# A conv and expert-layer kernel: one image pair's x is added to the experts' sum on PE and copied out by ACT

## What is computed

```python
x = x + conv_ref(_ln_c(x), conv_w, conv_b)      # _ln_c: norm over the channels of a pixel
t = _to_tokens(x)                               # a token is a pixel's 64 channels
t = t + ffn_ref(_ln_t(t), router_w, router_b, expert_w, expert_b)
# conv_ref: x * sigmoid(conv3x3([max over channels, mean over channels]))
# ffn_ref:  softmax router, best 2 of 8 experts, their two outputs mixed by the two probabilities
```

## Time and profile before

| | us |
|---|---|
| median of 3 runs | 1394.77 (1394.36 to 1395.02) |
| the profiled execution | 1395.69 |
| its span, first to last instruction | 1393.8 |

### The profile page before, as it was taken

The page is one execution under the profiler, slowest core; times in us unless marked ns, Lnnn a source line. Parts: engine busy times, 40 slices in busy tenths (PEclk is TensorE's granted clock), DMA queues, the critical chain, the costliest instruction groups (busy, mean ns, idle before and its releaser), DMA issues.

```text
span 1393.8 us, 33104 instructions
## 1 busy us (share of the span) xinstructions
PE 1294.6 (93%) x11750; PEld 612.6 (44%) x11750; DVE 1240.0 (89%) x1527; ACT 1052.0 (75%) x3950; POOL 1066.0 (76%) x643
## 2 busy tenths in 40 slices
PE   8964999999999999999999999999999898889998
PEld 8853444444444444444444444444444332333332
DVE  6787799988999899998999799998999879998887
ACT  5677898888998889888898889888898533444442
POOL 5333787887888787877878878878878878789885
PEclk9955999999999999999999999999999999999999
DMA  6443466676666666576666666676666555657774
GB/s 224 120 123 89 132 207 206 174 224 199 198 187 213 194 204 199 173 226 199 199 200 199 199 200 200 187 217 192 207 203 175 163 166 162 175 167 205 205 204 144
DMA packets 85845, 259.97 MB, mean 187 GB/s; under 512 B 13744, under 2 KB 13744, under 8 KB 85680
## 3 DMA queue, kind: packets, MB, share of 16 engines
q1 hardware_dynamic: 85680, 257.85, 62.0%
HBM read 206.42 MB, written 51.38 MB: 185 GB/s over the span
## 4 chain that ended last, share of the span: by engine, by line
PE 56%; DVE 23%; issue 9%; POOL 2%; ACT 2%; DVEq 0%; POOLq 0%; ACTq 0%
PE moe L568 34%; DVE gx L714 13%; PE tm L493 8%; PE gb L514 8%; PE tm L507 2%; DVE ge L736 2%; DVE stats L691 2%; PE moe L562 2%; PE tm L553 2%; DVE ot L727 1%; DVE oh L749 1%; PE tm L592 1%; DVE u L799 1%; POOL dl L1265 1%; ACT sq L965 1%
## 5 line engine op out<-in xcount | busy, mean ns | idle before, releaser
L568 PE MATMUL moe<-gx,wc 128*64 128x448 f32 x3584 | 803.5, 551 | 0.0
L714 DVE TENSOR_TENSOR gx<-gb,xd 128x896 f32<-128x896 f32 x672 | 710.7, 1086 | 77.3 <-PE gb L514 72.9
L1205 POOL TENSOR_TENSOR gx<-gs,xd 128x896 f32<-128x896 f32 x224 | 492.8, 2200 | 228.0 <-ACT gs L1003 158.7
L965 ACT ACTIVATE sq<-xct 112x64 f32<-112x64 f32 x1400 | 338.4, 246 | 7.5 <-DVE early_s L701 2.1
L1003 ACT ACTIVATE gs<-gb 128x896 f32<-128x896 f32 x224 | 205.3, 916 | 176.4 <-PE gb L514 170.9
L568 PEld LDWEIGHTS moe<-gx,wc 128*64 128x64 f32 x3584 | 219.9, 136 | 201.6 <-issue 159.2
L965 ACT ACTIVATION_READ_ACCUMULATOR sq<-xct 112x1 f32 x1400 | 265.5, 190 | 0.0
L1222 POOL TENSOR_TENSOR tt<-xc,a1s 128x896 f32<-128x896 f32 x112 | 235.1, 2099 | 11.3 <-issue 9.7
L514 PE MATMUL gb<-s,cg 32*128 32x448 f16 x1792 | 175.6, 358 | 53.2 <-DVE gx L714 51.8
L514 PEld LDWEIGHTS gb<-s,cg 32*128 32x128 f16 x1792 | 48.0, 91 | 383.2 <-DVE gx L714 348.7
L493 PE MATMUL tm<-rhs,xa 64*112 64x74 f32 x2800 | 184.6, 272 | 10.6 <-ACT early_l L950 5.2
(11 more groups left out here) (94 smaller groups left out, 1090.0 us busy)
## 6 DMA issues: line engine op xcount, KB each, us to landing
xd<-in_x_dram SPq DMA_DIRECT2D x448, 224.0 KB, 4.0
xa<-in_x_dram SPq DMA_DIRECT2D x112, 448.0 KB, 4.5
xc<-in_x_dram SPq DMA_DIRECT2D x112, 448.0 KB, 4.8
out_dram<-ot SPq DMA_DIRECT2D x112, 448.0 KB, 3.6
gx<-in_const_g_dram SPq DMA_DIRECT2D x1, 384.0 KB, 5.5
cf<-in_const_f_dram SPq DMA_DIRECT2D x1, 333.5 KB, 3.1
cf<-in_L_ffn_expert_b_dram SPq DMA_DIRECT2D x12, 1.0 KB
gx<-in_L_ffn_expert_w_dram SPq DMA_DIRECT2D x1, 128.0 KB, 5.3
```

Source lines behind the costliest of these rows:

```text
L568: last = pe.matmul(moe[b * CH:(b + 1) * CH, c, 0:HALF], wc[:, k * CH:(k + 1) * CH], gx[:, u, b, :], start=False, stop=(k == KT - 1), skip_ ...
L714: dve.tensor_tensor(gx[:, i, :, :], gb[:, 2 * slot:2 * slot + 2, 0:HALF], xd[:, v % 2, :, c * HALF:(c + 1) * HALF], ALU.mult).then_inc(sca ...
L965: last = act.activation(sq[:, n, :], xct[:, step % 2, n, :], ACT.Square, accum_out=to[:, 1, lo + n:lo + n + 1])
L1205: pool.tensor_tensor(gx[:, ND + j, :, :], gs[:, j, :, :], xd[:, v % 2, :, j * HALF:(j + 1) * HALF], ALU.mult).then_inc(scaled_p, 1)
```

## The change

For the blocks of pair 6 alone (the 14 steps from `LONE` on), DVE's `finish` is left out, for both sums. PE gets one more step of accumulation into `moe` for each sum, right behind the last unit of the sum (unit 2, unit 5): a multiplication of `tt` with a unit matrix in f32, two matmuls of 128x64 by 448 columns, which wait for POOL's `tt`. ACT gets a copy of the finished sum from `moe` to `ot`, which waits for that addition: for the second sum of v-1 right behind the copy P1, for the first sum of v right behind the copy P0 of v+1, ahead of the sigmoid and of `a1s`. Those who waited for DVE's count (`store`, `biases`, `scale_x`) wait for ACT's in these blocks. The unit matrix is 128 more columns of f32 in the first constant load `cf`. All other pairs are as before.

```diff
+    f[:, o + P + 2:] = np.eye(P)
-        cf = sb("cf", [P, CC + 3 * W + E + P + 2])
+        cf = sb("cf", [P, CC + 3 * W + E + P + 2 + P])
+        unit = cf[:, bias_c + P + 2:bias_c + P + 2 + P]
...
+        LONE = (PAIRS - 2) * STEPS
+        def lone_step(r, v):
+            return (r - 2) * STEPS + v - LONE
+        def by_act(r, v):
+            return 0 <= lone_step(r, v) < STEPS
+        def finished(eng, r, v, n):
+            step = (r - 2) * STEPS + v
+            if by_act(r, v):
+                eng.wait_ge(final_act, 2 * lone_step(r, v) + n)
+            elif step >= 0:
+                eng.wait_ge(final, 2 * (step if step < LONE else step - STEPS) + n)
...
+            def add_x(r, v, c):
+                if due(count := c_at(r, 1, v, 1)):
+                    pe.wait_ge(scaled_x, count)
+                for b in range(2):
+                    last = pe.matmul(moe[b * CH:(b + 1) * CH, c, 0:HALF], unit[:, b * CH:(b + 1) * CH],
+                                     tt[:, v % 2, c * HALF:(c + 1) * HALF],
+                                     start=False, stop=True, skip_group_check=True)
+                last.then_inc(added, 1)
             def experts_of_dve(r, v, i):
...
-                experts(i, D_PAIR[i], i // 3)
+                at_end = i % 3 == 2
+                experts(i, D_PAIR[i], i // 3, at_end and not by_act(r, v))
+                if at_end and by_act(r, v):
+                    add_x(r, v, i // 3)
...
-                    if on(r, v - 1):
+                    if on(r, v - 1) and not by_act(r, v - 1):
                         finish(r, v - 1, 1)
...
+                    if cur and not by_act(r, v):
                         finish(r, v, 0)
...
+            def finish(r, v, c):
+                sl = v % 2
+                act.wait_ge(added, 2 * lone_step(r, v) + c + 1)
+                if c == 0:
+                    if due(count := slot_at(r, v - 2, 16)):
+                        act.wait_ge(stored[sl], count)
+                act.activation(ot[:, sl, c * HALF:(c + 1) * HALF], moe[:, c, 0:HALF], ACT.Copy).then_inc(final_act, 1)
...
                     if cur:
                         gate_to_sbuf(r, v, 1)
+                    if by_act(r, v - 1):
+                        finish(r, v - 1, 1)
                     if parting:
                         part_one(r, v + 2)
...
                     if ahead:
                         gate_to_sbuf(r, v + 1, 0)
+                    if by_act(r, v):
+                        finish(r, v, 0)
                     if Bp and step == 2:
                         gate_of_conv(r)
```

More of the change, by code:

```diff
@@ L103, in constant_arrays @@
 def constant_arrays():
-    f = np.zeros((P, CC + 3 * W + E + P + 2), np.float32)
+    f = np.zeros((P, CC + 3 * W + E + P + 2 + P), np.float32)
     for b in range(2):
@@ L265, in gated_expert_program @@
         final = sem("final")
+        added = sem("added")
+        final_act = sem("final_act")
         FIRST_LOADS, LOADS, BIAS_LOADS = 3 * 16, 5 * 16, 12 * 16
@@ L407, in store @@
             def store(r, pairs, v):
-                if due(count := c_at(r, 2, v, 2)):
-                    sp.wait_ge(final, count)
+                finished(sp, r, v, 2)
                 pair = pairs[2] if v >= 0 else pairs[3]
@@ L558, in biases @@
             def biases(r, v, c):
-                if due(count := c_at(r, 2, v - 1, c + 1)):
-                    pe.wait_ge(final, count)
+                finished(pe, r, v - 1, c + 1)
                 for b in range(2):
@@ L564, in biases, with experts @@
                               start=True, stop=False, skip_group_check=True)
-            def experts(u, k, c):
+            def experts(u, k, c, last_of_all):
                 for b in range(2):
                     last = pe.matmul(moe[b * CH:(b + 1) * CH, c, 0:HALF], wc[:, k * CH:(k + 1) * CH],
-                                     gx[:, u, b, :], start=False, stop=(k == KT - 1), skip_group_check=True)
+                                     gx[:, u, b, :], start=False, stop=last_of_all, skip_group_check=True)
                 last.then_inc(mixed, 1)
+            def add_x(r, v, c):
[6 more added lines that the diff above has]
+                last.then_inc(added, 1)
             def experts_of_dve(r, v, i):
@@ L579, in experts_of_pool @@
                     pe.wait_ge(scaled_p, count)
-                experts(ND + j, P_PAIR, j)
+                experts(ND + j, P_PAIR, j, False)
             def convolve(r, A):
@@ L1219, in scale_x @@
                     pool.wait_ge(a1_out, count)
-                if due(count := c_at(r, 2, v - 2, 2)):
-                    pool.wait_ge(final, count)
+                finished(pool, r, v - 2, 2)
                 pool.tensor_tensor(tt[:, sl, :], xc[:, sl, :], a1s[:, sl, :], ALU.mult).then_inc(scaled_x, 1)
```

## The result

The changed kernel takes 1407.99 us (median of 4 runs, 1407.77 to 1408.20) against 1394.57 (4 runs): 13.4 us more, a ratio of 1.0091 (95% interval 1.0078 to 1.0103). The forecast was 1408.5. The profiled execution took 1408.2 with a span of 1406.4.

What follows compares the result with a forecast made beforehand. Round 8's halves are set by PE or by the router with the DVE-PE-DVE trip, not DVE's total work. 7.66 (steps 3 to 13) + 2.0 + 3.75 + 0 + 0.3 = 13.7 on 1394.77 gives 1408.5 us, range 1404 to 1413.

Steps and rivals of the forecast that it cites:

- What bounds round 8: Steps 3 to 13: PE or the router with a DVE-PE-DVE trip sets each half; hidden copy-outs worth 0 to 0.02 us.
- The price of an addition: 0.75 us where PE sets the half: 4.82 from unit 0's scaling to unit 2's, then 6.91 to the next step.
- Step 2: Round 8: the spread of a1 waits for the sigmoid behind ACT's copy, +2.0 us, bounds 0.75 and 2.2.
- the sigmoid's share: Step 2 of round 8: the sigmoid held behind ACT's copy, 1.25 us of the +2.0.
- Round 9: Five additions fall where PE has no gap: 5 x 0.75 = 3.75 us.
- The turns of DVE and POOL: Round 8: router operations on DVE and POOL take turns; 0 for steps 6 and 7, -0.67 us for step 11.
- Step 11: Round 8: `key` starts after POOL's `tt`, costing about 0.6 less: -0.67 us, 0 if the turns stay.
- steps 6 and 7: Round 8, 24.36 us together: DVE's later start only shortens its wait for POOL: 0, at most +0.75.
- what POOL does is tied to gx0: Steps 6 and 7: POOL's work follows gx0, the start of unit 0's scaling on DVE; lengthening taken as 0.
- ACT and the queues: 28 copies of 0.55 us on ACT, `parts` late but hidden by 0.35: 0; otherwise 0.15 in twelve steps, 1.8.
- The start: The constant load grows by 64 KB on 333.5 KB: 0 to 0.6 us, taken as 0.3.

Runs made afterwards that it cites:

- The kernel without additions: Changed kernel without PE's additions, ACT copying the experts' sum alone (x's share missing in pair 6): 1396.3 us against 1394.48 for the kernel before.
- the f16 additions: Changed kernel with POOL writing pair 6's gated x in f16 and the existing f16 unit matrix: 1398.14 us against 1395.09 for the kernel before.
- the order changed alone: Changed kernel with ACT's sigmoid ahead of its copy of the first sum in step 2: 1407.67 us against 1395.09 for the kernel before.
- the move of the router's work and the relief of DVE: Kernel before with round 8's router work on DVE behind units 1 and 4, nine of 28 sums on PE (f16) and ACT: 1391.59 us against 1395.23.
- the move alone: Kernel before with only round 8's router work on DVE moved behind units 1 and 4, copy-out still DVE's: 1394.14 us against 1395.23.
- the kernel with the router in the trip: Half precision kernel, sigmoid ahead of the copy, router's DVE work behind units 1 and 4 from step 3 of round 8: 1393.38 us against 1395.09.
- the kernel with the copy-out twice: Kernel before with DVE's addition for pair 6 done twice, the first into a spare buffer: 1399.01 us against 1395.09.

## Why the prediction was right

- *What bounds round 8.* Right, and against the shares: DVE at 95% was not the bound. The kernel without additions took 22 copy-outs off DVE in steps 3 to 13 and won 0.18 us there; the forecast for that was 0 to 0.02 a half.
- *The price of an addition.* Right: halves of 4.83 and 6.91, forecast 4.82 and 6.91. The 0.19 that the prediction estimates from the matmul row of the Trainium skill ("VectorE: DVE Perf Modes", section on the TRN2 errata) is what the f16 additions cost (0.19 to 0.20 a half, 4.28 and 6.35); for f32 the experts' rows were the ones to go by. The Trainium skill's page "FP8 and Floating Point Precision", section "TensorE Precision Notes", says that true f32 takes four passes, by which I estimate 4 x 0.19 = 0.76 from the f16 halves, beside 0.75 in the trace.
- *Step 2.* Right: 2.03 for 2.0, and the sigmoid's share, by the order changed alone, 1.28 for 1.25.
- *Round 9.* Right: 3.76 for 3.75.
- *The turns of DVE and POOL.* Half right. Step 11 came out as forecast (-0.64 for -0.67). For steps 6 and 7 I took 0 and it was -0.54. The failed step is "what POOL does is tied to gx0": in the kernel before, POOL comes into step 6 behind time, working without a gap from 1147.49 to 1163.4, and the longer step 5 lets it catch up. Its `lg` starts 5.7 us after gx0 (1166.57 from 1160.88), in the kernel before 6.5 (1161.66 from 1155.19). So `ge` takes 1.53 instead of 3.09, `tt` ends at 1173.71, just after `key` starts at 1173.63, and `key` takes 0.61 instead of 1.27: step 7 does what step 11 does. Step 6 before, then after:

```profile
1161.28 3.09 DVE L736 TENSOR_TENSOR ge<-lg,top 112x896 bf16<-112x896 f32 x1
1161.66 1.76 POOL L1244 TENSOR_TENSOR lg<-logit_mean,rho 112x896 f32<-112x896 f32 x1
...
1166.57 1.73 POOL L1288 TENSOR_TENSOR lg<-logit_mean,rho 112x896 f32<-112x896 f32 x1
1167.72 1.53 DVE L768 TENSOR_TENSOR ge<-lg,top 112x896 bf16<-112x896 f32 x1
```

- *ACT and the queues.* The copies take 0.54 us and `parts` was never late (POOL never stands idle for it in round 8): PE's halves have no other lengthening than the 0.75. The 0.15 a step that the prediction set aside for a late `parts` has no working in it, and no run shows such a cost.
- *The start.* Forecast +0.3, not seen: PE's first matmul starts at 5.83 us in place of 6.05, with a load of 397.5 KB that lands in 3.1 us as the smaller one did. What is left over between the stretch (13.05) and the medians (13.4) is smaller than what executions differ by ahead of round 8, so it stays open; the two profiled executions alone differ by 12.5. That the medians (13.4) lie nearer to the forecast (13.7) than the stretch does is luck as far as is known: the 0.3 forecast for the start and the unexplained 0.35 happen to be of one size.

The terms measured are 2.03, 7.26 and 3.76, in all 13.05 against 13.41 forecast without the start; the whole difference is the 0.54 of steps 6 and 7, less small change.

## What to carry to other kernels

An engine that is busy 95% of a stage is not its bound as long as part of its work lies inside a round trip that it would have to wait out anyway: before taking work off an engine, ask what the next instruction on it waits for, and put starts beside each other, not shares. Work that is given to an in-order engine costs in full in each stretch which that engine sets, so move only the pieces that fall where it has to wait. And a gap that is freed is worth something only if other work of the same engine can be put into it: here the move of the router's work and the relief of DVE won 4.6 us together, where the relief alone won 0.18 in steps 3 to 13 and the move alone 0.83, or 2.45 without the half in which the clock fell.

## What the runs showed of the hardware

DVE operations with both inputs in SBUF and POOL's operations take turns. `key` (112x896 bf16) takes 0.61 to 0.62 us when it starts at the end of POOL's `tt` or later and 1.27 when it starts 0.8 us ahead of that end; `dl` takes 1.09 and, in the kernel with the router in the trip, 2.87, where it starts at 1216.91 beside POOL's `q` (2.50 from 1216.33). So a longer step can shorten the next one, by up to 0.8 us here.

The early rounds, the same instructions in all kernels, do not take the same time in each profiled execution. The windows of the first 60 us hardly differ; in those of 60 to 160 us the granted clock is 0.64 or 0.61, and with 0.61 fewer instructions fall into them. Before, then the kernel with the copy-out twice:

```profile
60.00:160.00 100.00, 64.70 (x605) 50.67 (x607) 72.07 (x107) 70.87 (x293) 42.52 (x28) 0.64 0.32 91
```

```profile
60.00:160.00 100.00, 65.17 (x592) 50.83 (x594) 70.39 (x105) 69.13 (x286) 40.75 (x28) 0.61 0.30 87
```

In the seven executions with 0.64 the gx0 that ends step 0 of round 8 starts at 1098.7 to 1100.1 us, in the five with 0.61 at 1100.4 to 1101.5. Both levels of the clock, 1.2 and 2.4 GHz, occur in that stretch (in the kernel before 0.50 from 102 to 136 us, full up to 68); why the mean differs was not tried. In all, these starts lie up to 2.75 us apart, with the clock or without it, which is as much as the smaller experiments are about and is why they were read by stretch. In round 8 the clock fell once, in step 8 of the kernel with the move alone, and cost 1.62 us.
